# A fused decoder layer: the start of its attention, with other norms and another order for the first two batches

## The chip, the cores and the metric

The kernel runs on one core of a Trainium2 chip. A core has five engines that work beside each other, each through its own instructions in order, and they wait for each other by semaphores: TensorE (PE in the profile; PEld is its loading of stationary operands), VectorE (DVE), ScalarE (ACT), GpSimd (POOL) and SyncE (SP), which here only issues DMA transfers. Operands lie in SBUF, 128 partitions wide; PE writes into PSUM, eight banks of 512 fp32 columns per partition. The metric is the device time of one execution in microseconds, lower is better; the median of several executions is compared.

## What is computed

The input is x (8 batches, 256 rows, 512 columns, fp32) and a context of the same shape. Three blocks are added to x one after the other; only the first is touched:

```
x = x + attention(layernorm(x))         # 16 query heads in 4 groups, head size 32
x = x + long_convolution(ctx, ctx, layernorm(x))
x = x + quantised_ffn(layernorm(x))

attention(h):
    Q = rmsnorm_per_head(h @ Wq)        # 512 x 512
    V = h @ Wv                          # 512 x 128, 4 heads of 32
    K = rmsnorm_per_head(V)             # keys are the normalised values
    p = softmax(Q K^T)                  # the mask of the reference is never true
    return rmsnorm((p V) @ Wo)
```

The layer norm isn't applied to x. Its mean is taken out by subtracting from the weights their column means (or, for batch 0, from x itself its row means), and its scale falls out of the norm of each head, except that the small constant inside the square root has to be multiplied by the row's variance. So every head needs (mean square + constant x variance) to the power -1/2: 20 values a row (4 key heads, 16 query heads), 40 a partition for the 256 rows of a batch.

## The kernel before

The kernel is written by hand for each engine: what an engine does, and in which order, is the order of calls in its function, and the order between engines is in the semaphores. Attention goes through the batches in turns. Turn i computes the scores and outputs of batch i and, in between, projects the values v and queries q of batch i+1, so that their norms and copies can go on beside the scores.

A turn on PE (`turn`, L319 to L357) interleaves 16 scores (L274, one matmul each of 512 columns, in two PSUM banks by turns) with v(i+1) (L237, two tiles of 4 matmuls with 128 columns; the profile counts an fp32 matmul as two records) and q(i+1) (L243, 8 matmuls with 512 columns): scores 0 and 1, v and score 2, v and score 3, then eight times q and a score. `sum_weights` (L294) adds up the exponentials over the keys with a matrix of ones, `sum_values` (L306) multiplies them by the values. Then come the transposes of the next q (L255) and k (L261), and the output projection (L314). Score n can begin when ScalarE has taken the exponential (L435) of score n-2, and every other one of the first eight when its head group of q has been copied: SyncE copies the high and low halves of the transposed q into another layout (L176, 16 transfers per batch, four per head group).

Ahead of the turns stands a prologue for batch 0. SyncE issues the loads in this order: x's columns of batch 0, Wv, Wq, x's rows of batch 0, x's columns of batch 1, the other rows, Wo. PE then does, in this order (L359 to L377):

- `column_sums` of x's columns with a matrix of ones (L228), by which VectorE subtracts the mean from them (`centre`, L529, four instructions)
- v(0) and q(0), with the weights as they are
- `column_sums` of Wv and of Wq, by which VectorE subtracts their column means (`centre` again, one instruction for Wv, four for Wq)
- the transposes of q and k of batch 0
- waits for the centred weights (`c_wv`, `c_wq`), and turn 0.

VectorE meanwhile (L662 to L687) computes the row variances of batch 0, the low part of k (`k_low`, L534), the sums of squares of each head (`qk_sums`, L543, one for each half of the rows, from ScalarE's squares, L411), the norms (`qk_norms`, L546 to L564), the normalised q (`q_normalise`, L569), k's scales, q's low half (`q_low`, L584), then the two centrings, the row variances of batch 1, and turn 0.

`qk_norms` forms the variances in PSUM (L549) and takes the inverse root in eleven steps of 40 columns each: two on integers for a first guess, then three rounds of Newton's method. They are counted on one semaphore, `s_nr`, up to 11:

```python
for k in range(3):
    wait(dve, s_nr, i, 3 * k + 2)
    nc.vector.tensor_tensor(gr, ve2, rqk[:], ALU.mult).then_inc(s_nr.sem, 1)
    wait(dve, s_nr, i, 3 * k + 3)
    nc.vector.scalar_tensor_tensor(nt, gr, -0.5, rqk[:], ALU.mult, ALU.mult).then_inc(s_nr.sem, 1)
    wait(dve, s_nr, i, 3 * k + 4)
    nc.vector.scalar_tensor_tensor(rqk[:], nt, 1.5, rqk[:], ALU.add, ALU.mult).then_inc(s_nr.sem, 1)
```

GpSimd (L732 to L743) makes the identity matrix, raises the row variances to the power -1/2 (`power`, L700, two columns; in the last block, L1452, one column), scales the values of batch 0 (`values`, L708), and in its turns adds pairs of exponentials (`add_weights`, L717) for the sums of the weights.

v(1) waits for x's columns of batch 1, and for the first halves of q's high and low parts (`s_qhi`, `s_qlo`), because it writes the PSUM bank from which they are read.

Of the kernel before, what the change touches and what calls it, by code (L numbers as in the profile page):

```python
# [68 lines left out]
def wait(eng, signal, turn, n):  # L69
    eng.wait_ge(signal.sem, signal.at(turn, n))  # L70
# [12 lines left out]
def spread(ap, n):  # L83

    return ap[:, :, None].broadcast_to([ap.shape[0], ap.shape[1], n])


def attention(nc, ctx, m, x, xt, ctxt, wq, wv, wo, ssm, dskip, wall, krows):
# [136 lines left out]
    def _(pe):  # L225
        def column_sums(bank, w, done):
            for k in range(CK):
                mm = pe.matmul(bank, m.ones[:], w[:, k, :], start=(k == 0), stop=(k == CK - 1))  # L228
            mm.then_inc(done.sem, 1)
# [36 lines left out]
        def scores(i, n):  # L266
            kv, s, gp = score(n)
            if n < 2 * HKV and s == 0:
                wait(pe, d_qx[kv], i, 4 * 16)
            if n in (0, HKV):  # L270
                wait(pe, s_kx, i, kv // 2 + 1)
            if n >= 2:
                wait(pe, s_e, i, n - 1)
            pe.matmul(SB[:, n % 2, :], kx[:, kv, s * P:(s + 1) * P].bitcast(F32R),  # L274
                      qx[:, kv, gp * C:(gp + 1) * C].bitcast(F32R), start=True, stop=True).then_inc(s_sc.sem, 1)
# [35 lines left out]
        def project(i, k):  # L311
            wait(pe, s_y, i, max(k, 1))
            for t in range(TT):
                mm = pe.matmul(OB[:, t, :], yt[:, k, t * P:(t + 1) * P], wo_s[:, k, :],  # L314
                               start=(k == 0), stop=(k == CK - 1))
                if k == CK - 1:
                    mm.then_inc(s_wo.sem, 1)

        def turn(i, has_prev=True, has_next=True):  # L319
            scores(i, 0)  # L320
            scores(i, 1)
            for t in range(TT):
                if has_next:
                    v(i + 1, t)
                scores(i, 2 + t)
            for n in range(TT * CK):
                if has_next:
                    q(i + 1, n // CK, n % CK)
                if n == 6:
                    sum_weights(i, 0, has_prev)  # L330
                scores(i, 4 + n)
            scores(i, 12)
            sum_values(i, 0, 0, has_prev)
            scores(i, 13)
            sum_values(i, 0, 1, has_prev)
            scores(i, 14)
            if has_prev:
                q2_transpose(i - 1, 0, has_next)
            scores(i, 15)
            for s in range(TT):  # L340
                sum_values(i, 1, s, has_prev)
            sum_weights(i, 1, has_prev)
            if has_next:
                q_transpose(i + 1, after=has_prev)
            if not has_prev:
                pe.wait_ge(d_wo.sem, 16)
            for k in range(2):
                project(i, k)
            if has_next:
                k_transpose(i + 1)  # L350
            else:
                pe.wait_ge(c_sum.sem, 1)
                pe.matmul(MB[:, 0, 0:3], m.ones[:], wsum[:], start=True, stop=True).then_inc(c_tot.sem, 1)
            if has_prev:
                q2_transpose(i - 1, 1, has_next)
            for k in range(2, CK):
                project(i, k)  # L357
# [2 lines left out]
        pe.wait_ge(d_xt0.sem, 16)  # L360
        column_sums(OB[:, 0, 0:T], xt_first, c_xsum)
        pe.wait_ge(d_wv.sem, 16)
        pe.wait_ge(c_xc.sem, CK)
        for t in range(TT):
            v(0, t, rows=xt_first)
# [1 line left out]
        for n in range(TT * CK):  # L367
            q(0, n // CK, n % CK, rows=xt_first)

        column_sums(SB[:, 1, 0:P], wv_s, c_wvsum)  # L370
        column_sums(SB[:, 0, :], wq_s, c_wqsum)
        pe.wait_ge(c_ident.sem, 2)
        q_transpose(0, after=False)
        k_transpose(0)
        pe.wait_ge(c_wv.sem, 1)
        pe.wait_ge(c_wq.sem, CK)
        turn(0, has_prev=False)  # L377
        with pe.Fori(1, B - 2) as i:
            turn(i)
        turn(B - 2)  # L380
# [125 lines left out]
    def _(dve):  # L506
# [24 lines left out]
        def k_low(i):  # L531
            wait(dve, s_khi, i, 1)
            wait(dve, s_vn, i, 1)
            nc.vector.tensor_tensor(kparts[:, :, 1, :, :].bitcast(F32R),  # L534
                                    TB[:, 0, 0:TT * P].rearrange("p (n d) -> p n d", d=DH)[:, :, None, :]
                                    .broadcast_to([P, NV, 2, DH]),
                                    kparts[:, :, 0, :, :], ALU.subtract).then_inc(s_klo.sem, 1)

        def qk_sums(i, t, after=False):
            wait(dve, s_sq, i, t + 2)  # L540
            if after:
                wait(dve, s_q2e, i - 3, 2)
            nc.vector.tensor_reduce(ssq[:, t, :], sq[:, t, :].rearrange("p (n d) -> p n d", d=DH),  # L543
                                    AX.X, ALU.add).then_inc(s_ssq.sem, 1)

        def qk_norms(i):  # L546
            wait(dve, s_ssq, i, 2)
            wait(dve, s_ev1, i, 1)
            nc.vector.scalar_tensor_tensor(ve2, ssq, 1.0 / DH, spread(ev1[:], NH), ALU.mult, ALU.add  # L549
                                           ).then_inc(s_ve2.sem, 1)  # L550
            wait(dve, s_ve2, i, 1)

            nc.vector.tensor_scalar(nt.bitcast(I32), ve2.bitcast(I32), 1, None, ALU.logical_shift_right
                                    ).then_inc(s_nr.sem, 1)
            wait(dve, s_nr, i, 1)
            nc.vector.tensor_scalar(rqk[:].bitcast(I32), nt.bitcast(I32), -1.0, RSQRT_GUESS, ALU.mult, ALU.add
                                    ).then_inc(s_nr.sem, 1)
# [7 lines that stand above are left out]
# [105 lines left out]
        dve.wait_ge(d_x0.sem, 16)  # L670
        rows_var(0, first=True)
        k_low(0)
        for t in range(TT):
            qk_sums(0, t)
        qk_norms(0)
        q_normalise(0)
        k_scales(0, first=True)
        q_low(0)
        centre(wv_s[:], SB[:, 1:2, 0:P].broadcast_to([P, CK, P]), c_wvsum, c_wv)
        for k in range(CK):  # L680
            centre(wq_s[:, k, :], SB[:, 0, :], c_wqsum, c_wq)
        dve.wait_ge(d_x1.sem, 16)
        rows_var(1)
        dve.wait_ge(d_k.sem, 32)
# [11 lines left out]
    @block.gpsimd  # L696
    def _(pool):
        def power(out, var, signal_in, signal_out, i):
            wait(pool, signal_in, i, 1)
            nc.gpsimd.tensor_tensor(out[:], var[:], half[:], ALU.pow).then_inc(signal_out.sem, 1)  # L700

        def values(i, first=False):
            wait(pool, s_vn, i, 1)
            if not first:
                wait(pool, s_pv, i - 1, 2)
            wait(pool, s_rs1, i, 1)
            apart(pool)
            nc.gpsimd.tensor_tensor(vo[:], vn[:], spread(rs1[:], P), ALU.mult).then_inc(s_vo.sem, 1)  # L708

        def add_weights(i, n, has_prev):  # L710
            gp, kv = n // HKV, n % HKV
            wait(pool, s_e, i, 2 * (n + 1))
            if n == 6:
                wait(pool, s_den, i, 1)
            elif n == 0 and has_prev:
                wait(pool, s_den, i - 1, 2)
            nc.gpsimd.tensor_tensor(pts[:, n % 6, :], pt[:, 0, kv, gp * C:(gp + 1) * C],  # L717
                                    pt[:, 1, kv, gp * C:(gp + 1) * C], ALU.add).then_inc(s_ps.sem, 1)

        def turn(i, has_prev=True, has_next=True):  # L720
            if has_prev:
                power(ro, ve3, s_ve3, s_ro, i - 1)
            add_weights(i, 0, has_prev)
            if has_prev:
                power(rs4, ve4, s_ve4, s_rs4, i - 1)
            for n in range(1, 2 * HKV):
                add_weights(i, n, has_prev)
            if has_next:
                power(rs1, ve1, s_ve1, s_rs1, i + 1)
                values(i + 1)  # L730

        nc.gpsimd.memset(m.ident[:], 0.0).then_inc(c_ident.sem, 1)  # L732
        pool.wait_ge(c_ident.sem, 1)
        nc.gpsimd.affine_select(out=m.ident[:], in_=m.ident[:], compare_op=ALU.not_equal, fill=1.0, base=0,
                                pattern=[[-1, P]], channel_multiplier=1).then_inc(c_ident.sem, 1)
        pool.wait_ge(c_half.sem, 1)
        power(rs1, ve1, s_ve1, s_rs1, 0)
        values(0, first=True)
        turn(0, has_prev=False)
        with pool.Fori(1, B - 2) as i:  # L740
            turn(i)
        turn(B - 2)
        turn(B - 1, has_next=False)  # L743

        wait(pool, s_sc, B - 1, 16)
        for r in range(2):
            pool.wait_ge(m.d_ctx[r].sem, 16)
            context_products(nc, m, r, 0).then_inc(m.s_kv.sem, 1)
        power(ro, ve3, s_ve3, s_ro, B - 1)
        power(rs4, ve4, s_ve4, s_rs4, B - 1)  # L750
# [846 lines left out]
```

## Time and profile before

| | us |
|---|---|
| median of 3 executions | 643.58 (642.78 to 644.29) |
| the profiled execution | 645.77 |
| its span in the profile | 643.9 |
| PE busy | 586.8 |
| DVE busy | 485.7 |
| ACT busy | 456.1 |
| POOL busy | 362.8 |

The profile records start and duration of every instruction of one execution. The mean clock granted to PE is 0.976 of the full one. Times below count from the start of the span. "x16" stands for 16 instructions that the view has put together; matmul ends are modelled, and a matmul's record can begin while the one before still streams.

### The profile page before, as it was taken

The numbers are of one execution on the slowest core, as the hardware profiler recorded it, in microseconds if no ns is written. First come the engines' busy times: TensorE is split into PE (matmuls) and PEld (weight loads), VectorE is DVE, ScalarE is ACT, GpSimd is POOL, SyncE is SP. The second block draws the span as 40 slices with busy tenths as digits, with TensorE's granted clock in tenths as the row PEclk, the third lists the DMA queues.
The fourth block names the chain that finished last, engine by engine and source line by source line (L and its number), as shares of the span: only waits on it lengthen the run. The fifth ranks groups of instructions, "written<-read, shape, count | busy, mean of one in ns | idle before, by whom it ended". The sixth has DMA issues, their size and how long they took to land. (4 is left out here: it accounts for less than half of the span.)

```text
span 643.9 us, 9966 instructions
## 1 busy us (share of the span) xinstructions
PE 586.8 (91%) x2569; PEld 326.7 (51%) x2586; DVE 485.7 (75%) x938; ACT 456.1 (71%) x781; POOL 362.8 (56%) x324
## 2 busy tenths in 40 slices
PE   6789999999999996979999999999789999999975
PEld 4353444545353542357777777765334444444332
DVE  2528687787887785437787789988999889989861
ACT  1254667677677665258889888889788888898971
POOL 1033535262725435537777777765667777778771
PEclk9979999999999997899999999999899999999998
DMA  8593337465454736025666655643153344533424
GB/s 287 202 251 81 87 92 219 114 195 130 163 131 162 179 116 155 25 78 175 163 192 175 179 181 166 172 151 100 41 92 99 92 105 98 122 98 77 95 66 114
DMA packets 88955, 87.26 MB, mean 136 GB/s; under 512 B 46880, under 2 KB 62752, under 8 KB 88928
## 3 DMA queue, kind: packets, MB, share of 16 engines
q1 hardware_dynamic: 88928, 86.94, 49.9%
q8 instruction: 12, 0.20, 0.1%
q14 instruction: 15, 0.12, 0.1%
HBM read 51.71 MB, written 4.28 MB: 87 GB/s over the span
## 5 line engine op out<-in xcount | busy, mean ns | idle before, releaser
L785 PE MATMUL ps<-kv,toep 128*128 128x288 f32 x640 | 158.0, 407 | 3.6 <-DVE big L830 1.3
L785 PEld LDWEIGHTS ps<-kv,toep 128*128 128x128 f32 x640 | 120.6, 190 | 40.3 <-issue 4.3
L1182 PE MATMUL ps<-wt,xqt 128*128 128x512 bf16 x496 | 118.0, 383 | 13.4 <-DVE toep L1351 11.8
L717 POOL TENSOR_TENSOR pts<-big 128x512 f32<-128x512 f32 x64 | 85.1, 1340 | 61.0 <-ACT big L435 60.7
L435 ACT ACTIVATE big<-ps,kscale 128x512 f32<-128x512 f32 x128 | 85.6, 687 | 44.0 <-PE ps L274 41.8
L1456 POOL TENSOR_TENSOR big<-toep,wst 128x512 f32<-128x512 f32 x64 | 82.8, 1296 | 46.6 <-DVE toep L1351 45.8
L1182 PEld LDWEIGHTS ps<-wt,xqt 128*128 128x128 bf16 x512 | 49.0, 98 | 74.9 <-DVE toep L1351 16.0
L274 PE MATMUL ps<-qx,kx 128*128 128x512 f32 x128 | 77.5, 630 | 10.0 <-DMA qx<-kv 8.1
L838 DVE TENSOR_REDUCE qo<-big 128x256 f32<-128x2048 f32 (+1 forms) x32 | 72.2, 2258 | 0.0
L594 DVE RECIPROCAL yt<-ps 128x256 f32<-128x256 f32 (+1 forms) x24 | 54.8, 2284 | 20.4 <-PE ps L294 20.4
L773 POOL TENSOR_TENSOR kv<-ctx 128x768 f32<-128x768 f32 (+1 forms) x32 | 52.7, 1647 | 28.9 <-PE ps L785 23.9
L1170 PE MATMUL ps<-wt,act8t 128*128 128x512 bf16 x255 | 59.5, 387 | 9.3 <-DMA act8t<-ys 8.3
L877 POOL TENSOR_TENSOR big<-ys,qd 128x768 f32<-128x768 f32 x32 | 56.4, 1764 | 17.8 <-ACT ys L921 14.3
L243 PE MATMUL ps<-wq_s,qo 128*128 128x512 f32 x128 | 65.7, 604 | 0.0
L827 DVE TENSOR_TENSOR big<-ps,qd 128x1024 f32<-128x1024 f32 x32 | 39.1, 1223 | 30.5 <-ACT ys L921 27.2
L314 PE MATMUL ps<-wo_s,yt 128*128 128x512 f32 x128 | 57.9, 594 | 0.0
L274 PEld LDWEIGHTS ps<-qx,kx 128*128 128x128 f32 x128 | 25.1, 200 | 55.7 <-issue 32.8
L1213 ACT ACTIVATE kv<-ps 128x512 f32<-128x512 f32 x64 | 37.7, 589 | 16.1 <-PE ps L1182 16.1
L700 POOL TENSOR_TENSOR ro<-ve,half 128x2 f32<-128x2 f32 x8 | 5.5, 692 | 76.8 <-DVE ve L605 76.8
L1351 DVE TENSOR_TENSOR toep<-ps,kv 128x512 f32<-128x512 f32 x64 | 43.6, 682 | 4.8 <-ACT kv L1215 4.6
L1170 PEld LDWEIGHTS ps<-wt,act8t 128*128 128x128 bf16 x256 | 24.4, 99 | 42.6 <-DMA act8t<-ys 13.0
L1224 ACT ACTIVATE asq<-toep 128x512 f32<-128x512 f32 x64 | 39.7, 621 | 6.3 <-DVE sm L1361 4.0
(124 smaller groups left out, 971.7 us busy)
## 6 DMA issues: line engine op xcount, KB each, us to landing
qx<-kv SPq DMA_DIRECT2D x128, 128.0 KB, 2.4
wst<-in_wall SPq DMA_DIRECT2D x12, 1024.0 KB, 6.4
wst<-in_wall SPq DMA_DIRECT2D x48, 256.0 KB, 3.5
toep<-krows SPq DMA_DIRECT2D x32, 256.0 KB, 3.5
ctx<-in_ctxt SPq DMA_DIRECT2D x32, 192.0 KB, 2.5
qo<-in_xt SPq DMA_DIRECT2D x8, 512.0 KB, 3.9
out_y<-ot SPq DMA_DIRECT2D x16, 256.0 KB, 2.2
conv_part<-qo SPq DMA_DIRECT2D x14, 256.0 KB, 2.9
```

Source lines behind the costliest of these rows:

```text
L243: mm = pe.matmul(MB[:, t, :], rows[:, k, t * P:(t + 1) * P], wq_s[:, k, :], start=(k == 0), stop=(k == CK - 1))
L274: pe.matmul(SB[:, n % 2, :], kx[:, kv, s * P:(s + 1) * P].bitcast(F32R), qx[:, kv, gp * C:(gp + 1) * C].bitcast(F32R), start=True, stop=Tr ...
L314: mm = pe.matmul(OB[:, t, :], yt[:, k, t * P:(t + 1) * P], wo_s[:, k, :], start=(k == 0), stop=(k == CK - 1))
L435: act.activation(pt[:, s, kv, gp * C:(gp + 1) * C], SB[:, n % 2, :], ACT.Exp, scale=kscale[:, c:c + 1]).then_inc(s_e.sem, 1)
L594: nc.vector.reciprocal(y[:, gp * C + a:gp * C + b], weight_bank[gp][:, a:b]).then_inc(s_rd.sem, 1)
L717: nc.gpsimd.tensor_tensor(pts[:, n % 6, :], pt[:, 0, kv, gp * C:(gp + 1) * C], pt[:, 1, kv, gp * C:(gp + 1) * C], ALU.add).then_inc(s_ps.s ...
L785: mm = pe.matmul(m.ps[:, LB * r + lb, :].rearrange("p (b s) -> p b s", s=WIDE)[:, :, 0:PAIRS], m.toep[r][:, d * P:(d + 1) * P], m.kv[r][:, ...
L838: nc.vector.tensor_reduce(qo[:, :, bass.ds(h * HD, HD)], z[r][:], AX.X, ALU.add).then_inc(s_red.sem, 1)
L877: nc.gpsimd.tensor_tensor(z[r][:, :, :, HD - SHIFTS:HD].rearrange("p n j s -> p n s j"), window(ys[r][:], SHIFTS - 1, (SHIFTS * EW, NB), ( ...
L1170: mm = pe.matmul(DB, act8t[r][:, k, :], down_w[:, k, :], start=(k == 0), stop=(k == FK - 1))
L1182: mm = pe.matmul(bank[:, n % 2, :], xqt[r][:, k, :], wt[:, k, n * C:(n + 1) * C], start=(k == 0), stop=(k == CK - 1))
L1456: nc.gpsimd.tensor_tensor(act_w[r][:, n * C:(n + 1) * C], a[n % 2][:], gain_at(n), ALU.mult).then_inc(s_w.sem, 1)
```

## The change

Three edits, all ahead of turn 1.

1. The norms of batch 0: the variances go into SBUF in place of PSUM, and GpSimd raises all 40 columns to -1/2 in one instruction, in place of VectorE's eleven steps. It stands in GpSimd's queue behind the scaling of batch 0's values and signals `s_nr` by 11 at once. The other batches keep `qk_norms`.
2. The column sums of Wv move on PE from behind q(0) to ahead of v(0), and the centring of Wv on VectorE from behind `q_low(0)` to behind `k_low(0)` (it overwrites Wv, which v(0) has read by then). The column sums of Wq stay, in another PSUM bank (`OB[:, 1, :]` in place of `SB[:, 0, :]`).
3. Turn 0 on PE gets an order of its own: v(1) whole ahead of score 0, the wait for the centred Wq behind score 1, then eight times q(1) and a score, from score 2 on. `sum_weights` stands behind score 10 instead of ahead of it. From score 12 on the order is as before (`second_half`). ScalarE, VectorE and SyncE keep their order in turn 0.

```diff
+        def first_turn():
+            for t in range(TT):
+                v(1, t)
+            scores(0, 0)
+            scores(0, 1)
+            pe.wait_ge(c_wq.sem, CK)
+            for n in range(TT * CK):
+                q(1, n // CK, n % CK)
+                scores(0, 2 + n)
+            scores(0, 10)
+            sum_weights(0, 0, False)
+            scores(0, 11)
+            second_half(0, has_prev=False)
...
                 scores(i, 4 + n)
+            second_half(i, has_prev, has_next)
+
+        def second_half(i, has_prev=True, has_next=True):
             scores(i, 12)
...
         pe.wait_ge(d_wv.sem, 16)
+        column_sums(SB[:, 1, 0:P], wv_s, c_wvsum)
         pe.wait_ge(c_xc.sem, CK)
...
-        column_sums(SB[:, 1, 0:P], wv_s, c_wvsum)
-        column_sums(SB[:, 0, :], wq_s, c_wqsum)
+        column_sums(OB[:, 1, :], wq_s, c_wqsum)
         pe.wait_ge(c_ident.sem, 2)
         q_transpose(0, after=False)
         k_transpose(0)
         pe.wait_ge(c_wv.sem, 1)
-        pe.wait_ge(c_wq.sem, CK)
-        turn(0, has_prev=False)
+        first_turn()
...
+        def first_variances():
+            wait(dve, s_ssq, 0, 2)
+            wait(dve, s_ev1, 0, 1)
+            nc.vector.scalar_tensor_tensor(rqk[:], ssq, 1.0 / DH, spread(ev1[:], NH), ALU.mult, ALU.add
+                                           ).then_inc(s_ve2.sem, 1)
...
         k_low(0)
+        centre(wv_s[:], SB[:, 1:2, 0:P].broadcast_to([P, CK, P]), c_wvsum, c_wv)
         for t in range(TT):
             qk_sums(0, t)
-        qk_norms(0)
+        first_variances()
         q_normalise(0)
         k_scales(0, first=True)
         q_low(0)
-        centre(wv_s[:], SB[:, 1:2, 0:P].broadcast_to([P, CK, P]), c_wvsum, c_wv)
         for k in range(CK):
-            centre(wq_s[:, k, :], SB[:, 0, :], c_wqsum, c_wq)
+            centre(wq_s[:, k, :], OB[:, 1, :], c_wqsum, c_wq)
...
         values(0, first=True)
+        wait(pool, s_ve2, 0, 1)
+        nc.gpsimd.tensor_tensor(rqk[:], rqk[:], spread(half[:], NH), ALU.pow).then_inc(s_nr.sem, 11)
         turn(0, has_prev=False)
```

## Rows read from the trace of the kernel before

**Rows 1.** The page: busy time, share of the span, instructions of PE.

```profile
PE 586.8 (91%) x2569; PEld 326.7 (51%) x2586; DVE 485.7 (75%) x938; ACT 456.1 (71%) x781; POOL 362.8 (56%) x324
```

**Rows 2.** Timeline 4 to 17 us: start, us, engine, line, operation, out<-in [idle before <-releaser].

```profile
4.82 3.75 PE L228 MATMUL ps<-qo,ones 128*128 128x256 f32 x8 [4.82 <-DMA qo<-in_xt]
...
10.18 3.75 PE L237 MATMUL ps<-wv_s,qo 128*128 128x128 f32 x16 [1.60 <-DVE qo L529]
...
13.72 8.31 PE L243 MATMUL ps<-wq_s,qo 128*128 128x512 f32 x16
...
14.23 0.17 DVE L519 TENSOR_SCALAR ve<-mv 128x2 f32<-128x2 f32 x1
...
14.55 0.72 POOL L700 TENSOR_TENSOR rs<-ve,half 128x2 f32<-128x2 f32 x1 [13.08 <-DVE ve L519]
...
15.43 0.34 PEld L243 LDWEIGHTS ps<-wq_s,qo 128*128 128x128 f32 x1 [0.52 <-issue]
16.29 0.19 PEld L243 LDWEIGHTS ps<-wq_s,qo 128*128 128x128 f32 x1 [0.52 <-issue]
16.72 0.19 PEld L243 LDWEIGHTS ps<-wq_s,qo 128*128 128x128 f32 x1 [0.24 <-issue]
```

**Rows 3.** Timeline 21 to 35 us: the norms of batch 0 and the first scores.

```profile
21.87 1.05 PE L228 MATMUL ps<-wv_s,ones 128*128 128x128 f32 x8
...
22.70 0.83 DVE L543 TENSOR_REDUCE ps<-sq 128x20 f32<-128x640 f32 x1 [2.60 <-ACT sq L411]
22.76 3.60 PE L228 MATMUL ps<-wq_s,ones 128*128 128x512 f32 x8
...
23.56 0.21 DVE L549 SCALAR_TENSOR_TENSOR ps<-ps,ev 128x40 f32<-128x40 f32 x1
...
26.43 1.29 DVE L569 TENSOR_TENSOR qn<-ps,rqk 128x512 f32<-128x512 f32 x2
...
27.27 1.16 PE L255 MATMUL ps<-ident,qn 128*128 128x128 f32 x8 [0.91 <-DVE qn L569]
...
28.26 1.04 PE L261 MATMUL ps<-ident,kparts 128*128 128x128 f32 x8
...
29.92 10.16 SPq L176 DMA_DIRECT2D qx<-kv  x16
...
34.47 1.19 PE L274 MATMUL ps<-qx,kx 128*128 128x512 f32 x2 [5.17 <-DMA qx<-kv]
```

**Rows 4.** Timeline of turn 0 and the start of turn 1.

```profile
35.46 1.91 PE L237 MATMUL ps<-wv_s,qo 128*128 128x128 f32 x8
...
42.59 0.80 PE L274 MATMUL ps<-qx,kx 128*128 128x512 f32 x1
...
48.57 3.36 DVE L594 RECIPROCAL yt<-ps 128x512 f32<-128x512 f32 x1 [2.02 <-PE ps L294]
...
65.65 1.02 PE L274 MATMUL ps<-qx,kx 128*128 128x512 f32 x2
...
66.51 1.05 PE L237 MATMUL ps<-wv_s,qo 128*128 128x128 f32 x8
```

**Rows 5.** DMA issues by line: count, KB each, median us from issue to landing.

```profile
wq_s<-in_wq SPq DMA_DIRECT2D x1, 1024.0 KB, 9.0
...
wv_s<-in_wv SPq DMA_DIRECT2D x1, 256.0 KB, 4.0
```

**Rows 6.** Busy time by stretches: length, each engine, granted PEclk, DMA share, GB/s.

```profile
33.00:34.00 1.00, 0.00 (x0) 0.00 (x0) 1.00 (x3) 0.00 (x0) 0.00 (x0) 0.67 0.91 205
...
40.00:41.00 1.00, 1.00 (x3) 0.44 (x3) 0.00 (x0) 1.00 (x2) 0.27 (x1) 0.91 0.92 201
```

**Rows 7.** GpSimd by line and form: busy us, mean ns of one, idle before.

```profile
L717 POOL TENSOR_TENSOR pts<-big 128x512 f32<-128x512 f32 x64 | 85.1, 1340 | 61.0 <-ACT big L435 60.7
...
L700 POOL TENSOR_TENSOR rs<-ve,half 128x2 f32<-128x2 f32 x16 | 11.2, 703 | 29.3 <-DVE ve L519 29.3
L1452 POOL TENSOR_TENSOR r<-var,fhalf 128x1 f32<-128x1 f32 x16 | 8.7, 543 | 1.3 <-DVE var L1366 1.3
```

## The prediction

> **What bounds the kernel now.** I read the page first, then the granted clock by stretches, then the instructions in order of time up to the second turn of the attention loop. The page puts TensorE (PE) at 91% of the span [rows 1], so the kernel is bound by PE's order of work nearly everywhere. The change touches only the first 45 us, and there it is different: PE is waiting in two places. The first wait lies between the sums of x's columns and the first values: PE stops at 4.82 + 3.75 = 8.57 us and goes on at 10.18, after VectorE (DVE) has centred x [rows 2]. The second is a chain. q(0) ends at 22.03 [rows 2]; ScalarE squares it, DVE reduces it until 23.53, forms the variances, and runs eleven steps of an inverse root until it can start normalising at 26.43. PE, done with the sums of wq's columns at 26.36, transposes from 27.27. SyncE starts the copies of q at 29.92, and the first scores begin at 34.47, when the first four copies have landed [rows 3]. I call that instant T. What comes later moves with T, so the sum goes by two questions: when is T, and how long is it from T to the next turn's first scores, now 65.65 - 34.47 = 31.18 us [rows 3, 4]?
>
> **Part 1, wv's sums into the first gap.** Eight matmul records, the first row of [rows 3], leave their place behind q(0) and stand ahead of v(0). wv's load is the second that SyncE issues, right behind that of x's columns, which had landed by 4.82; it takes 4.0 us to land [rows 5], so it is there before 8.57. One such record takes 3.75 / 16 = 0.234 us in v(0) [rows 2] and 1.05 / 8 = 0.131 us in the next turn [rows 4]: two levels of the clock, 1.2 and 2.4 GHz. The page's slices say 1.00 for this stretch, but the spacing of q(0)'s weight loads shows the truth: 0.86 us from 15.43 to 16.29, then 0.43 [rows 2]. PE rose to 2.4 GHz at about 16.3, that is 6.1 us after it took up unbroken work at 10.18. The second rise says the same: granted 0.91 in the microsecond from 40 [rows 6], so it rose near 40.2, 5.7 us after T. In the changed kernel PE works without a break from 4.82. By these two rows I put its rise at 4.82 + 5.9 = 10.7 us (an estimate). Then the sums end at 8.57 + 8 x 0.234 = 10.45, 0.27 later than v(0) starts today. v(0) runs until 10.45 + 0.25 + 15 x 0.131 = 12.7, and q(0) with 16 x 0.43 = 6.88 until 19.6. wq has landed by then (issue to landing 9.0 us, and q(0) follows v(0) without a break today) [rows 2, 5]. **q(0) ends 2.45 us earlier.** If the rise came no earlier, it would end 0.3 us later than now. wv's centring on DVE goes ahead of the first reduction, where DVE waits for ScalarE's square of q(0) in both kernels; only the second reduction sets the end. wq's sums move to another PSUM bank, whose next writer comes late in the turn: nothing.
>
> **Part 2, one power for eleven steps.** Reduction and variances stay (0.21 us) [rows 3]. Gone are the steps between 23.77 and 26.43. In their place DVE signals GpSimd (0.15 us, from 14.40 to 14.55 [rows 2]), GpSimd raises 40 columns to a power, and DVE goes on. Its queue holds nothing in the way: the scaling of the first values is done long before, and the next addition waits for the second exponential, after T. Everything hangs on the power's time p, and the trace has none with 40 columns. It has 16 over one column at 543 ns and 16 over two at 703 [rows 7]. So p is 0.70 at the least, if further columns cost nothing, and 0.54 + 39 x 0.16 = **6.8 us** if each costs what the second did. For a plain addition on GpSimd 512 columns take 1.34 us [rows 7], 2 to 3 ns a column, so the 0.16 us is not the reading of an operand but the arithmetic of the power itself, and I see no reason why it should shrink with more columns. I take 6.6, just under the straight line, because GpSimd's spans are rough. The reduction then ends at 23.53 - 2.45 = 21.08, the variances at 21.32, the power at 28.07, and DVE normalises at 28.1: **1.65 us later than today**, although q came 2.45 earlier.
>
> The Trainium skill (GPSIMD Engine Reference, sections 1 and 3.1) gives a clock of 1.2 GHz and about 2.6 cycles an element for a two-operand operation: 38 more columns would be 0.08 us, p about 0.8 (an estimate from the page). The page states this for an addition; the rows agree for the addition and not for the power. By that rule the sum is the first rival's lower end.
>
> **Part 3, PE meanwhile.** wq's sums end at 19.6 + 3.6 = 23.2 and the transposes start 0.84 after DVE, as today [rows 3], at 28.9. Today PE rests from the last transposes of k, 29.3, to T [rows 3], and the granted clock fell at about 33.3 [rows 6]; so in a rest of 5.7 us I let it fall here too. Eight transposes take 8 x 0.235 instead of 1.16 [rows 3], which delays the second low half of q, and with it the copies, by 0.75. **T is 34.47 + 1.65 + 0.75 = 36.9.**
>
> **Part 4, v(1) ahead of the scores.** Behind the transposes of k (until 32.7) v(1) needs at most 16 x 0.234 = 3.75 us, to 36.5: hidden by the copies, and PE is at 2.4 GHz when the scores start. (Were that cover gone, v(1) would cost 2.1 us at the high clock.) Today v(1) takes 2 x 1.91 us between the scores at half clock [rows 4]. What is late next is the copies: sixteen issues in 10.16 us, so the fourth head group lands 7.6 us after T, against 42.59 - 34.47 = 8.12 at which PE asks for it today [rows 3, 4]. From there today's order has rounds of one q (2 x 0.43) and one score, some 1.1 us each, until the reciprocal of the weight sums starts at T + 14.1 [rows 4]. In the new order q is interleaved from the third score on, two such q's are done by then, and the sums come after score 10: s6 at T + 7.6, three rounds to score 9 at T + 10.9, score 10 and the sums until T + 12.5. DVE's chain (reciprocal, second norms, normalising) is 1.5 us shorter against T; PE's own, through scores 12 to 15, some 2.4 or more. The second transposes now wait for DVE instead of PE, the outputs for both, and I take **2.1 us less from T to the next first scores**. wq's centring must now be done only before q(1), and it was done before T; SyncE's later loads keep their place behind the copies.
>
> **The sum.** +1.65 + 0.75 - 2.1 = +0.3 us on the profiled execution, 645.77 to 646.1. That execution is 2.2 above the median of 643.58. Its v(1) at half clock costs 2 x (1.91 - 1.05) = 1.7 us of that by itself, and an execution whose clock did not fall before T is faster by this. The changed kernel starts its scores at the high clock in either case, so its executions lie closer together and its median nearer to 646.1 than to 643.9. I take **645.3**, 1.7 us (0.27%) slower than the median before. A measurement of this kernel can tell about 0.2%, 1.3 us, from no change.
>
> **Rivals.** *A: further columns are cheap* (0.30). p lies between 0.7 and 4 us. At half the slope, p = 3.6, DVE normalises at 25.1, PE rests under 3 us and keeps its clock: -1.3 - 2.1 = -3.4, about 641.5 by the same reading of the median. At 0.7 wq's sums bind instead: transposes at 23.3, four earlier, -6.1, some 639. For it: a loop may overlap columns once it has many. Against: the only step the trace shows, from one to two, is 160 ns. *B: it evens out* (0.25), 642.3 to 644.9: p of 5 to 6, or the idle PE keeps its clock (0.75 back), or the second half of the turn gains 2.5. *C: PE's clock does not rise early* (0.10). The wv sums are short records with a weight load each, as v(0) has, and v(0), from 10.18 to 13.7, ran at the low level throughout. Then q(0) ends at 22.3, the chain is 2.75 later, 648. It decides if q(0)'s first weight loads still stand 0.85 apart.
>
> **Chances.** Forecast 0.35: 644.9 to 646.9, p of 6.2 to 7.2. Faster than 642.3 is A, 0.30. Within 0.2% is B, 0.25. Slower is the forecast and C, 0.45. The range goes from 640.5, about p = 2.5, to 647.0: it leaves out A's lower end and most of C. The forecast's own range is 644.4 to 646.7.
>
> **What would show it.** The row of a power over 128x40 on GpSimd: 6 to 7 us, or the forecast falls. Weight loads of q(0) 0.43 apart from the first on, and q(0) ending near 19.6. Normalising near 28.1, T near 36.9, v(1) wholly ahead of it. From T to the reciprocal of the first weight sums 12.5 us, to the next first scores 29.1. A time under 642.3 with p over 6 would mean that parts 1 and 4 gained over twice what I give them.

## The result, and the profile after

The changed kernel takes 647.15 us, the median of 20 executions (644.31 to 649.28); the kernel before, timed beside it, 644.0 (641.15 to 647.6, 20 executions). The ratio is 1.0047, with a 95% interval of 1.0029 to 1.0066: **slower by 3.0 us, 1.9 to 4.3.** The forecast was slower by 1.7 us, at 645.3; the measured time lies 0.15 us above its range. (The kernel before was itself 0.4 us slower here than the 643.58 from which the forecast was counted.)

The profiled execution of the changed kernel is one of its fastest, 644.46 us with a span of 642.5, less than the 643.9 of the kernel before. PE is busy for 585.5 us of it, against 586.8 [rows 1]. A pair of profiles would have said "faster". The timeline of the changed kernel, first 66 us (columns as in [rows 2]):

```profile
8.46 1.08 PE L228 MATMUL ps<-wv_s,ones 128*128 128x128 f32 x8
...
10.17 2.05 PE L237 MATMUL ps<-wv_s,qo 128*128 128x128 f32 x16 [0.62 <-DVE qo L545]
...
12.05 7.03 PE L243 MATMUL ps<-wq_s,qo 128*128 128x512 f32 x16
...
18.93 3.60 PE L228 MATMUL ps<-wq_s,ones 128*128 128x512 f32 x8
...
20.62 0.20 DVE L565 SCALAR_TENSOR_TENSOR rqk<-ps,ev 128x40 f32<-128x40 f32 x1
20.96 6.76 POOL L762 TENSOR_TENSOR rqk<-rqk,half 128x40 f32<-128x40 f32 x1 [6.12 <-DVE rqk L565]
27.75 1.29 DVE L591 TENSOR_TENSOR qn<-ps,rqk 128x512 f32<-128x512 f32 x2 [6.93 <-POOL rqk L762]
28.59 1.94 PE L255 MATMUL ps<-ident,qn 128*128 128x128 f32 x8 [6.07 <-DVE qn L591]
...
32.02 2.13 PE L237 MATMUL ps<-wv_s,qo 128*128 128x128 f32 x16
...
36.32 0.73 PE L274 MATMUL ps<-qx,kx 128*128 128x512 f32 x2 [2.16 <-DMA qx<-kv]
...
49.13 3.36 DVE L616 RECIPROCAL yt<-ps 128x512 f32<-128x512 f32 x1 [1.41 <-PE ps L294]
...
65.53 1.03 PE L274 MATMUL ps<-qx,kx 128*128 128x512 f32 x2
```

This is the course that the prediction described. wv's sums fill the gap, v(0) runs at the high clock (2.05 us for 16 records against 3.75 [rows 2]), q(0) ends at 19.08 against 22.03. The power over 40 columns takes 6.76 us, DVE and PE wait for it (6.93 and 6.07 us idle), and DVE normalises at 27.75 against 26.43 [rows 3]. The transposes take 1.94 instead of 1.16: the clock fell in PE's rest. T is 36.32, v(1) lies wholly ahead of it, and the next turn's first scores start at 65.53, where the kernel before had 65.65 [rows 4]. So in this pair of executions the change comes out even at the end of turn 0, as the sum had said (+0.3). What the sum could not show is how far that one execution of the kernel before stands for the others.

### The profile page after: what moved, and what is told of

Its sections match the earlier page's. It is cut to its first block and busy times, and to the rows that moved or that the text cites. A ratio compares the mean times of both kernels' runs of the same rounds, so it can differ in the third digit from the quotient of the medians.

```text
span 642.5 us, 9973 instructions
## 1 busy us (share of the span) xinstructions
PE 585.5 (91%) x2586; PEld 325.3 (51%) x2586; DVE 483.6 (75%) x927; ACT 456.5 (71%) x781; POOL 369.4 (58%) x325
## 5 line engine op out<-in xcount | busy, mean ns | idle before, releaser
L1206 PEld LDWEIGHTS ps<-wt,xqt 128*128 128x128 bf16 x512 | 49.1, 98 | 73.8 <-DVE toep L1375 14.1
L274 PE MATMUL ps<-qx,kx 128*128 128x512 f32 x128 | 75.1, 614 | 8.0 <-DMA qx<-kv 6.1
L243 PE MATMUL ps<-wq_s,qo 128*128 128x512 f32 x128 | 64.2, 592 | 0.0
```

The source lines that it names most:

```text
L243: mm = pe.matmul(MB[:, t, :], rows[:, k, t * P:(t + 1) * P], wq_s[:, k, :], start=(k == 0), stop=(k == CK - 1))
L1206: mm = pe.matmul(bank[:, n % 2, :], xqt[r][:, k, :], wt[:, k, n * C:(n + 1) * C], start=(k == 0), stop=(k == CK - 1))
```

## The experiments

Below, S is the start of the next turn's first scores (65.65 and 65.53 in the two profiles).

**The parts alone.** One kernel has the reorderings without the power, one the power without the reorderings. The first, against the changed kernel:

```diff
-        first_variances()
+        qk_norms(0)
...
-        wait(pool, s_ve2, 0, 1)
-        nc.gpsimd.tensor_tensor(rqk[:], rqk[:], spread(half[:], NH), ALU.pow).then_inc(s_nr.sem, 11)
```

> The changed kernel with DVE's eleven steps put back for batch 0: only the two reorderings on PE and DVE are left. Theory P (the power costs 0.16 us a column, the two reorderings gain what the sum gave them): q(0) ends at 19.1 as in the changed kernel, DVE normalises at about 23.5 in place of 27.75, PE never rests long enough ahead of the transposes to lose its clock, first scores at about 31.5, next turn's first scores at about 60.7 against 65.65 before: about 4 us faster than the kernel before, 640. Rival H (the reorderings are hidden anyway, or harm): within 1 us of the kernel before, and the power would then cost only 3 us.

Measured: 643.05 us, ratio 0.9973 (0.9946 to 1.0000). Its trace has what was expected of it, DVE normalising at 23.43, first scores at 31.30, S at 60.57:

```profile
24.26 1.16 PE L255 MATMUL ps<-ident,qn 128*128 128x128 f32 x8 [1.80 <-DVE qn L585]
...
31.30 0.73 PE L274 MATMUL ps<-qx,kx 128*128 128x512 f32 x2 [2.89 <-DMA qx<-kv]
...
60.57 1.02 PE L274 MATMUL ps<-qx,kx 128*128 128x512 f32 x2
```

But the gain is 1.7 us instead of 4, and its interval (0 to 3.5) reaches down to nothing and doesn't reach 4.

The other takes these lines the other way round: the kernel before with `first_variances` and the power in place of `qk_norms(0)`.

> The kernel before with only the power on GpSimd in place of DVE's eleven steps. Theory P: DVE normalises at 23.53 + 0.4 + 6.8 = 30.7 in place of 26.43, PE rests 5 us more ahead of the transposes, so that its clock falls there in some executions; first scores at 38.7 to 39.5; 4.3 to 5 us slower than the kernel before, about 648.6. Rival H: 3 us slower at most, about 647, since the changed kernel is that much slower with reorderings that do nothing.

Measured: 650.65 us, ratio 1.0088 (1.0057 to 1.0119), 5.7 us slower. DVE normalises at 29.36, first scores at 38.13, S at 69.51:

```profile
22.58 6.75 POOL L746 TENSOR_TENSOR rqk<-rqk,half 128x40 f32<-128x40 f32 x1 [6.78 <-DVE rqk L549]
29.36 1.29 DVE L575 TENSOR_TENSOR qn<-ps,rqk 128x512 f32<-128x512 f32 x2 [6.93 <-POOL rqk L746]
...
69.51 1.02 PE L274 MATMUL ps<-qx,kx 128*128 128x512 f32 x2
```

Rival H falls: the power costs 3.7 us at the least, where H had 3 at most. The power is the whole loss, and the reorderings do help. But they help by less than the first profile promised.

**PE kept busy during the power.** Three more column sums of x into a bank that nobody reads.

```diff
         column_sums(OB[:, 1, :], wq_s, c_wqsum)
+        for _ in range(3):
+            for k in range(CK):
+                pe.matmul(OB[:, 0, 0:T], m.ones[:], xt_first[:, k, :], start=(k == 0), stop=(k == CK - 1))
```

> The changed kernel with 24 idle records of PE work (the column sums of x three times more, into a bank that nobody reads) behind the sums of Wq's columns, so that PE doesn't rest while GpSimd works on the power; they end at about 27.7, before the transposes can start. Theory P: the transposes run at the high clock, 0.75 us earlier copies, 646.4 against 647.15. Rival K (the loss beyond the sum, some 1.5 us, is PE's clock, which falls in every execution in this long rest and then delays more than the transposes): 645.5 or less, and the executions lie closer together than the 5 us of the changed kernel.

Measured: 647.09 us, ratio 1.0031 (1.0005 to 1.0057).

```profile
22.63 5.34 PE L391 MATMUL ps<-qo,ones 128*128 128x256 f32 x24
28.86 1.16 PE L255 MATMUL ps<-ident,qn 128*128 128x128 f32 x8 [0.89 <-DVE qn L594]
...
31.52 8.68 SPq L176 DMA_DIRECT2D qx<-kv  x13
...
36.25 0.74 PE L274 MATMUL ps<-qx,kx 128*128 128x512 f32 x2 [3.25 <-DMA qx<-kv]
...
65.60 1.02 PE L274 MATMUL ps<-qx,kx 128*128 128x512 f32 x2
```

The transposes take 1.16 us, the granted clock stays at 1.00 ahead of the scores, and from DVE's normalising (28.02) to the first scores (36.25) it is 8.23 us instead of 8.57. Of that nothing is left at S: 65.60, where the changed kernel's mean over six traces (below) is 65.59. The executions spread over 5.0 us as before. By these rows rival K falls; the timing alone doesn't exclude it, since K's 645.5 would be a ratio of 1.0023 to the 644.0 of the first timing.

**The kernel before, traced again.** The same kernel four times more.

> The kernel before once more, for its trace: the clock of PE stands otherwise against the start of the program than in the first profile. Theory P: first scores at 34 to 34.5 whatever the clock does, the next turn's first scores at 64.5 to 65.7. Rival K: an execution in which the clock doesn't fall ahead of the first scores reaches the next turn 2 us earlier, at 63.5.

> The kernel before once more, for its front alone: when does PE's clock rise, and when does q(0) end? So far 22.0, 20.5 (in e2_power_only, whose front is the same) and 19.0. Theory N: this and the two traces that follow have a mean below 20.5, with at least one early rise (9.5 or before, q(0) done by 19.1), and the first scores follow q(0)'s end by 12.4 to 12.7 us in each. Theory O: 21.5 to 22 in nearly all.

> The kernel before again, the second of three traces. Theory N: a mean end of q(0) below 20.5 over the three. Theory O: 21.5 to 22.

> The kernel before again, the third of three traces. Theory N: a mean end of q(0) below 20.5 over the three. Theory O: 21.5 to 22.

The first of these traces (644.56 us) shows the most. Its timeline, to be read against [rows 2 to 4]:

```profile
4.95 3.75 PE L228 MATMUL ps<-qo,ones 128*128 128x256 f32 x8 [4.95 <-DMA qo<-in_xt]
...
10.30 2.02 PE L237 MATMUL ps<-wv_s,qo 128*128 128x128 f32 x16 [1.60 <-DVE qo L529]
...
12.16 7.03 PE L243 MATMUL ps<-wq_s,qo 128*128 128x512 f32 x16
...
23.59 1.29 DVE L569 TENSOR_TENSOR qn<-ps,rqk 128x512 f32<-128x512 f32 x2
...
31.66 1.19 PE L274 MATMUL ps<-qx,kx 128*128 128x512 f32 x2 [5.20 <-DMA qx<-kv]
...
32.65 1.91 PE L237 MATMUL ps<-wv_s,qo 128*128 128x128 f32 x8
...
63.12 1.03 PE L274 MATMUL ps<-qx,kx 128*128 128x512 f32 x2
```

PE idles 1.6 us ahead of v(0) as ever, and yet v(0) runs at the high clock from its first record, 2.02 us for 16. Nothing was filled, and q(0) ends at 19.19, as early as in the changed kernel. Neither theory had this: T is 31.66, not P's 34 to 34.5, and S lies near K's 63.5, but v(1)'s first half takes 1.91 us, so the clock was low at T, and K's reason isn't there. The row of v(0) in the third, fourth and fifth trace, one after the other:

```profile
10.30 3.52 PE L237 MATMUL ps<-wv_s,qo 128*128 128x128 f32 x16 [1.60 <-DVE qo L529]
```

```profile
10.23 2.02 PE L237 MATMUL ps<-wv_s,qo 128*128 128x128 f32 x16 [1.60 <-DVE qo L529]
```

```profile
10.25 3.75 PE L237 MATMUL ps<-wv_s,qo 128*128 128x128 f32 x16 [1.60 <-DVE qo L529]
```

| trace of the kernel before | v(0), us | q(0) ends | T | S |
|---|---|---|---|---|
| the first profile | 3.75 | 22.03 | 34.47 | 65.65 |
| second | 2.02 | 19.19 | 31.66 | 63.12 |
| third | 3.52 | 20.68 | 33.15 | 63.62 |
| fourth | 2.02 | 19.12 | 31.57 | 62.14 |
| fifth | 3.75 | 21.18 | 33.62 | 64.35 |

The mean end of q(0) is 20.44; the first profile was the latest of the five. The new three have a mean of 20.33, and one of them is early, as theory N had it. In all five the first half of v(1) takes 1.91 us, so the clock was low at T in each: what the prediction took for the accident of one execution is the rule. What it took for the rule, a rise as late as 16.3, is the latest of five cases, whose q(0) ends up to 2.9 us apart.

**The changed kernel, traced again and timed again.**

> The changed kernel once more. Both theories: q(0) ends at 18.9 to 19.8, DVE normalises at 27.7 to 28.6, the power takes 6.7 to 6.8 us, the next turn's first scores at 65.3 to 66.5, and what comes behind them takes between 576 and 581 us by the half-clock stretches there, not by the change.

> The changed kernel again, timed beside the kernel before. By the traces so far the next turn's first scores stand 1.8 us later than in five traces of the kernel before (65.6 against a mean of 63.8), while the medians stood 3.15 apart (interval 1.9 to 4.2). Theory N: the ratio comes out between 1.0028 and 1.0045, and the front of this trace is like the two before: q(0) done at 18.9 to 19.4, next turn's first scores at 65.3 to 66.2. Rival F: in executions of the changed kernel that are slower than the two traced so far (644.5, 647.0) the front itself is later, 67 or more.

> The changed kernel again, for its trace. Theory N: next turn's first scores at 65.3 to 66.2, and what is left of the spread of its executions (644.3 to 649.3) lies behind them, 576 to 582 us. Rival F: first scores of the next turn at 67 or later in a slow execution.

> The changed kernel again, for its trace. Theory N: next turn's first scores at 65.3 to 66.2, the spread behind them. Rival F: at 67 or later in a slow execution.

> The changed kernel again, for its trace. Theory N: next turn's first scores at 65.3 to 66.2, the spread behind them. Rival F: at 67 or later in a slow execution.

The second timing gives 648.39 us and a ratio of 1.0040 (1.0016 to 1.0065), as theory N had it. In all six traces q(0) ends between 19.03 and 19.24, DVE normalises between 27.7 and 27.9, and S lies at 65.53, 65.72, 65.59, 65.56, 65.59 and 65.53. Rival F falls: the front is the same to 0.2 us whether the execution takes 644.5 or 648.8. What differs lies behind it. Two of them by stretches (columns as in [rows 6]); first the profiled execution of 644.46 us:

```profile
440.00:480.00 40.00, 32.51 (x147) 14.25 (x146) 37.66 (x89) 32.45 (x61) 25.97 (x24) 0.96 0.34 70
480.00:640.00 160.00, 145.46 (x672) 65.22 (x672) 130.49 (x372) 128.22 (x227) 111.33 (x102) 0.98 0.42 96
```

and that of 648.81 us:

```profile
440.00:480.00 40.00, 33.51 (x148) 15.15 (x146) 36.10 (x85) 32.56 (x61) 25.24 (x23) 0.91 0.28 68
480.00:640.00 160.00, 145.16 (x668) 64.79 (x667) 132.42 (x377) 129.39 (x229) 112.35 (x103) 0.97 0.43 97
```

The granted clock is 0.91 against 0.96 in the one stretch, 0.97 against 0.98 in the other, in code that the change doesn't touch; that the clock is the reason for the longer time isn't shown by that alone. From S to the end of the span the six traces take 577.0 to 580.3 us, the five of the kernel before 578.2 to 580.6.

**The clock brought up in both kernels.** Sixteen records on the matrix of ones from 1.1 us on, while PE waits for x's columns.

```diff
         pe.wait_ge(c_ones.sem, 1)
+        for _ in range(8):
+            pe.matmul(OB[:, 1, 0:P], m.ones[:], m.ones[:], start=True, stop=True)
         pe.wait_ge(d_xt0.sem, 16)
```

> The kernel before with eight products of the matrix of ones with itself (16 records, nobody reads them) on PE from 1.1 us until x's columns land, so that PE works without a break from 1.1 to the end of x's sums and its clock is high when v(0) starts, in every execution. Theory N (the clock of the kernel before rises at any time from 9 to 16.3 us, as three traces show: 16.3, 13.5, 9.2; the first profile, on which the sum was made, was the latest of them): q(0) ends at 18 to 19, first scores at 30.5 to 31.5; 1.3 to 2.5 us faster than the kernel before. Theory O (the clock rises late in nearly all executions of the kernel before, as in the first profile, and the changed kernel gains 2.45 us there, but loses 2.6 somewhere else): 3 to 4 us faster.

Measured: 643.23 us, ratio 0.9981 (0.9959 to 1.0003). q(0) ends at 17.87 and the first scores start at 30.33, both a little ahead of what N had; S is 61.83:

```profile
1.08 3.78 PE L361 MATMUL ps<-ones 128*128 128x128 f32 x16 [1.08 <-DVE magic L667]
4.80 1.99 PE L228 MATMUL ps<-qo,ones 128*128 128x256 f32 x8
8.39 2.02 PE L237 MATMUL ps<-wv_s,qo 128*128 128x128 f32 x16 [1.60 <-DVE qo L531]
...
61.83 1.02 PE L274 MATMUL ps<-qx,kx 128*128 128x512 f32 x2
```

It is 1.2 us faster (2.6 at the most), just under N's 1.3 to 2.5; O's 3 to 4 is excluded.

> The changed kernel with the same 16 records at the start. Both kernels now have their clock up before v(0), so what is left between this run and e5_before_front is the power against the eleven steps (+4.3), the transposes at the low clock (+0.75) and the order of turn 0 (-2.1). Theory N: 3 us slower than e5_before_front, at most 1 us faster than the changed kernel without them. Theory O: 5 to 5.6 us slower than e5_before_front.

Measured: 644.9 us, ratio 1.0024 (1.0000 to 1.0048). Between the two kernels with the same start there are 0.0043, 2.8 us (3.5 at S, 65.32 against 61.83), as N had it (3) and not as O (5 to 5.6). Against the changed kernel it is 1.0 to 1.5 us faster by the ratios, a little more than N allowed, though only 0.3 us earlier at S.

The same start in the kernel without the power:

> The two reorderings without the power, with the same 16 records at the start: first scores near 30.5 to 31, next turn's first scores near 60. Theory N: 2 us faster than e5_before_front by the order of turn 0 alone, 3.5 to 4.5 us faster than the kernel before, the fastest kernel so far. Theory O: the same against e5_before_front, 5 to 6 us faster than the kernel before.

Measured: 640.64 us, ratio 0.9941 (0.9914 to 0.9968): 3.8 us faster than the kernel before, as N had it, and **the fastest of all** by the median. From first scores (29.90) to S (59.13) it is 29.23 us.

```profile
6.65 1.05 PE L228 MATMUL ps<-wv_s,ones 128*128 128x128 f32 x8
...
8.32 2.05 PE L237 MATMUL ps<-wv_s,qo 128*128 128x128 f32 x16 [0.62 <-DVE qo L547]
...
22.03 1.29 DVE L587 TENSOR_TENSOR qn<-ps,rqk 128x512 f32<-128x512 f32 x2
22.86 1.16 PE L255 MATMUL ps<-ident,qn 128*128 128x128 f32 x8 [1.80 <-DVE qn L587]
...
24.98 2.02 PE L237 MATMUL ps<-wv_s,qo 128*128 128x128 f32 x16
...
29.90 0.73 PE L274 MATMUL ps<-qx,kx 128*128 128x512 f32 x2 [2.89 <-DMA qx<-kv]
...
59.13 1.02 PE L274 MATMUL ps<-qx,kx 128*128 128x512 f32 x2
```

PE waits 1.8 us for DVE's eleven steps here, and 6.07 for the power in the changed kernel.

**The gap alone.** wv's sums ahead of v(0), nothing else.

```diff
         pe.wait_ge(d_wv.sem, 16)
+        column_sums(SB[:, 1, 0:P], wv_s, c_wvsum)
         pe.wait_ge(c_xc.sem, CK)
...
-        column_sums(SB[:, 1, 0:P], wv_s, c_wvsum)
```

> The kernel before with wv's column sums alone moved from behind q(0) into the gap ahead of v(0). Theory N: the clock rises between 8.5 and 11 us in every execution instead of between 9 and 16.3; 1.2 us faster than the kernel before on the median, and executions that were fast before are no faster. Theory O: 2.45 us faster.

Measured: 644.17 us, ratio 0.9994 (0.9972 to 1.0015): 0.4 us, and 1.8 at the most.

```profile
8.43 1.92 PE L228 MATMUL ps<-wv_s,ones 128*128 128x128 f32 x8
10.15 2.14 PE L237 MATMUL ps<-wv_s,qo 128*128 128x128 f32 x16
...
62.96 1.02 PE L274 MATMUL ps<-qx,kx 128*128 128x512 f32 x2
```

The 2.45 us that the sum booked for it are excluded; N's 1.2 is not.

**All together.** S against the mean of the five traces of the kernel before (63.78), beside the difference in time that the ratio gives (times 644). Below the first row each S comes from one trace:

| kernel | S | S - 63.78 | timed |
|---|---|---|---|
| changed (mean S of six traces) | 65.59 | +1.8 | +3.0 (1.9 to 4.3), again +2.6 (1.0 to 4.2) |
| without the power | 60.57 | -3.2 | -1.7 (-3.5 to 0) |
| power alone | 69.51 | +5.7 | +5.7 (3.7 to 7.7) |
| changed, PE kept busy | 65.60 | +1.8 | +2.0 (0.3 to 3.7) |
| before, clock brought up | 61.83 | -2.0 | -1.2 (-2.6 to +0.2) |
| changed, clock brought up | 65.32 | +1.5 | +1.5 (0 to 3.1) |
| no power, clock brought up | 59.13 | -4.7 | -3.8 (-5.5 to -2.1) |
| gap alone | 62.96 | -0.8 | -0.4 (-1.8 to +1.0) |

The front tells the order of the kernels, to within 1.5 us; of the changed kernel's 3.0 it explains 1.8. The other 1.2 is not settled. It doesn't lie in the front of the changed kernel, which is constant, and the eleven traces don't hold it behind the front either: from S to the end the changed kernel takes 578.8 us on average, the kernel before 579.8. Three things can make it up:

- Five traces can put the mean S of the kernel before too late by some tenths. In no row is the timed difference clearly below the shift of S; on average it is 0.6 us above it.
- The clock behind S. The 30 timed executions of the changed kernel were granted 0.9729 on average, the 75 of the kernel before whose clock is on record 0.9752, and in both kernels a lower clock goes with a longer span, by 0.3 to 0.4 us for 0.001. The difference would be 0.7 to 0.8 us (an estimate). Up to 65 us all eleven traces were granted the same, 1.00, 0.86 and 1.00 in the stretches up to 20, 45 and 65 us, so it would lie behind them; why the clock should be lower there isn't shown.
- Chance, since 1.8 is just short of the first interval and within the second.

## Why the prediction was wrong in size

**Part 1 failed: "q(0) ends 2.45 us earlier".** For the changed kernel the step was right, 19.1 where 19.6 was said, and its clock rises at the place that was estimated or before it (in the profile the eight records of wv's sums, from 8.46, take 1.08 us, the high level). Wrong was what it was compared with. The first profile's rise at 16.3 is the latest of five; two of the others run all of v(0) at the high clock without any help. Against the mean of the five the gain is 20.44 - 19.11 = 1.3 us; the gap alone, timed, gave 0.4, with 1.3 inside its interval. The prediction had two rises to read from, both in the same execution, and made of them a property of the kernel and a place for the rise. In the second trace PE has just rested for 1.6 us when v(0) starts, and its clock is already up.

**The step from the profiled execution to the median failed with it.** The prediction saw that the profile stood 2.2 us above the median, and sought the cause in v(1) at half clock. That is there in every trace of the kernel before. What sets this execution's front apart is the late rise: its T of 34.47 is 2.9 us behind that of the fourth trace. That the late rise makes up the 2.2 isn't shown either, for the fourth trace is of an execution of 645.65 us, as long as the first profile's 645.77. The prediction also said that the executions of the changed kernel would lie closer together. In the front they do, 0.2 us of S against 3.5; in the whole time they hardly do (they spread over 5.0 us against 6.5 in the first timing, 5.3 against 4.8 in the second), because the spread behind the front stays.

**Part 2 was right.** 6.76 us for the power, between the 6.6 taken and the 6.8 of the straight line from one and two columns. The columns, from GpSimd's rows by line and form in the changed kernel:

```profile
L722 POOL TENSOR_TENSOR rs<-ve,half 128x2 f32<-128x2 f32 x16 | 11.4, 710 | 28.2 <-DVE ve L535 28.2
L1476 POOL TENSOR_TENSOR r<-var,fhalf 128x1 f32<-128x1 f32 x16 | 8.7, 544 | 1.3 <-DVE var L1390 1.3
...
L762 POOL TENSOR_TENSOR rqk<-rqk,half 128x40 f32<-128x40 f32 x1 | 6.8, 6756 | 6.1 <-DVE rqk L565 6.1
```

(6756 - 544) / 39 = 159 ns a column. Rival A, further columns for nothing, is out. By the Trainium skill's figure for an addition (GPSIMD Engine Reference, section 3.1) the power would have taken about 0.8 us, an estimate from the page; the row shows 6.76, and it decides. From q(0)'s end to DVE's normalising it is 8.67 us in the changed kernel and 4.40 in the kernel before: +4.27, as the sum had it (1.65 + 2.45 = 4.1).

**Part 3 was right in kind and 0.2 too dear.** The clock falls in PE's rest and the transposes take 1.94. SyncE starts the copies 4.21 us behind normalising, where it was 3.49 (29.92 - 26.43) [rows 3], so 0.72 later, as was said:

```profile
31.96 10.13 SPq L176 DMA_DIRECT2D qx<-kv  x16
```

But from there to T it is 4.36 us against 4.55, so that from normalising to T it is 8.57 against 8.04, +0.53 where 0.75 was said. In the run with PE kept busy the copies start as early as before (3.50 behind normalising), and T follows 4.73 us later. Why the first copies take shorter or longer to T wasn't examined.

**Part 4 was right.** From T to S it is 29.21 against 31.18, 2.0 us less where 2.1 was said; against the mean of the five traces, 30.88, it is 1.7. The reciprocal of the first weight sums comes 12.8 us behind T (12.5 said, 14.1 before).

**Rival C** (the clock doesn't rise early) does not occur in any of the six traces of the changed kernel. **Rival B** was the nearest to what the two profiles show, and would have been the wrong reading of them.

With 1.3 in place of 2.45 the prediction's own terms give 1.65 + 1.15 + 0.75 - 2.1 = +1.45 against an average execution; with the measured sizes, 4.27 - 1.33 + 0.53 - 1.67 = +1.8, which is the shift of S. That the forecast of +1.7 lies so close to it is luck: Part 1 booked 1.1 us too much, and the step to the median put 1.4 on top (from +0.3 to +1.7) for a reason that isn't there. The miss of the time is another matter. The measured 3.0 exceeds the forecast by 1.3 us, about what the front doesn't hold, and no part of the prediction that is known to be wrong accounts for that; its cause stays open.

## What to carry to other kernels

Before the price of a step is taken from one execution, look at what in it depends on PE's clock: the same prologue had its first scores anywhere from 31.6 to 34.5 us. A gain that consists of a clock that rises earlier must be measured against several executions, or the clock brought up in both kernels, which cost nothing here while PE waited for its first load (x's sums start at 4.80, 4.88 and 4.82 us with it, at 4.71 to 4.97 in the traces without it). And the power on GpSimd was priced rightly by the step from one column to two (160 ns, against 159 a column over forty), not by the cost of the call: over two columns it took 0.7 us, over forty 4 us more than the eleven steps on VectorE.

## What was not expected of the hardware

The profile's granted clock says 1.00 from the start, while PE's first records run at the low level; only their durations (0.234 us against 0.131 for the same record) show it. The same program has its clock up when v(0) starts at 10.3 us, or not before 16.3. Sixteen records on constants from 1.1 us on brought it up before v(0) in the three kernels that were traced with them: x's sums take 1.99 us in two of them and 3.17 in the third, against 3.75.
